# Cross attention on one core: the tail copy moved between exp and high part, and a third buffer for the low parts

## The reference

```python
q = (pre_q @ Wq + bq).reshape(b, ql, H, D_Q)
k = (pre_k @ Wk + bk).reshape(b, kl, H, D_Q)
v = (pre_k @ Wv + bv).reshape(b, kl, H, D_Q)
scores = jnp.einsum('bqhd,bkhd->bhqk', q, k) / jnp.sqrt(jnp.float32(D_Q))
attn = jax.nn.softmax(scores, axis=-1)
ctx = jnp.einsum('bhqk,bkhd->bqhd', attn, v).reshape(b, ql, H * D_Q)
out = ctx @ Wo + bo
x = pre_q + out
mu = jnp.mean(x, axis=-1, keepdims=True)
var = jnp.mean(jnp.square(x - mu), axis=-1, keepdims=True)
return (x - mu) * jax.lax.rsqrt(var + EPS) * gamma + beta
```

## Time and profile before

| | us |
|---|---|
| median of 3 runs (lowest, highest) | 908.91 (907.51, 912.77) |
| the profiled execution's own time | 911.81 |
| its span, first to last instruction | 909.9 |
| mean granted TensorE clock | 0.993 of full |
| TensorE matmuls busy | 882.5 |
| VectorE busy | 814.9 |
| ScalarE busy | 746.3 |
| GpSimd busy | 327.0 |

### The profile page before, as it was taken

How to read it: one execution, slowest core, us unless ns; L and a number is a source line. 1 busy time by engine, 2 the same in 40 slices (tenths; PEclk the granted TensorE clock), 3 DMA queues, 4 the chain that set the end, 5 groups by cost and what they waited for, 6 DMA issues and landing times.

```text
span 909.9 us, 25457 instructions
## 1 busy us (share of the span) xinstructions
PE 882.5 (97%) x10366; PEld 674.6 (74%) x10366; DVE 814.9 (90%) x1041; ACT 746.3 (82%) x1082; POOL 327.0 (36%) x385
## 2 busy tenths in 40 slices
PE   7799999999999999999999999999999999999996
PEld 6477777777777777777777777777777777777776
DVE  4799799999998999999899999989999899998983
ACT  3677868888888888888888888888888888888883
POOL 3032496434415234242514434143442435243011
PEclk9899999999999999999999999999999999999999
DMA  8598978999999999999999999999999999999995
GB/s 232 112 190 168 196 158 184 218 207 185 216 211 205 209 210 213 197 201 222 204 209 208 209 210 219 207 194 208 213 221 207 198 217 200 205 197 211 203 178 113
DMA packets 683065, 181.17 MB, mean 199 GB/s; under 512 B 654596, under 2 KB 682052, under 8 KB 682948
## 3 DMA queue, kind: packets, MB, share of 16 engines
q1 hardware_dynamic: 681332, 178.48, 103.7%
q10 hardware_dynamic: 1344, 0.53, 0.2%
q0 software_dynamic: 272, 0.53, 0.2%
HBM read 15.35 MB, written 0.82 MB: 18 GB/s over the span
## 4 chain that ended last, share of the span: by engine, by line
PE 34%; DVE 18%; ACT 15%; SPq 14%; DMA 11%; issue 8%; POOL 0%; POOLq 0%; ACTq 0%; DVEq 0%
PE ps L532 14%; PE ps L546 10%; DMA pt_lo<-p_lo 9%; DVE p_lo L767 8%; ACT p L861 6%; SPq L331 5%; DVE nmax L752 5%; PE ps L551 5%; ACT p_hi L869 5%; SPq L339 4%; PE ps L400 2%; ACT o_t L884 2%; DVE rsum L758 1%; SPq L323 1%; DMA pt_hi<-p_hi 1%
## 5 line engine op out<-in xcount | busy, mean ns | idle before, releaser
L869 ACT ACTIVATE p_hi<-p,rinv 128x1444 f16<-128x1444 f32 x200 | 299.8, 1499 | 89.3 <-DVE rinv L760 87.4
L767 DVE SCALAR_TENSOR_TENSOR p_lo<-p,rinv,p_hi 128x1444 f16<-128x1444 f32 x200 | 349.9, 1749 | 13.5 <-DMA pt_lo<-p_lo 10.7
L752 DVE TENSOR_REDUCE nmax<-ps 128x1 f32<-128x1446 f32 x200 | 329.8, 1649 | 8.7 <-PE ps L532 8.7
L861 ACT ACTIVATE p<-ps,nmax 128x1446 f32<-128x1446 f32 x200 | 291.7, 1459 | 26.3 <-DVE nmax L752 25.4
L546 PE MATMUL ps<-pt_hi,c_hi 128*128 128x128 f16 (+1 forms) x2288 | 268.7, 217 | 3.6 <-ACT o_t L884 3.1
L546 PE MATMUL ps<-pt_hi,c_lo 128*128 128x128 f16 (+1 forms) x2288 | 268.6, 217 | 0.0
L546 PEld LDWEIGHTS ps<-pt_hi,c_hi 128*128 128x128 f16 x2288 | 216.8, 98 | 34.4 <-ACT o_t L884 14.5
L546 PEld LDWEIGHTS ps<-pt_hi,c_lo 128*128 128x128 f16 x2288 | 217.0, 98 | 17.9 <-issue 0.2
L532 PE MATMUL ps<-ct_hi,g_hi 128*128 128x482 f16 (+3 forms) x624 | 157.1, 370 | 2.2 <-DMA ct_hi<-c_hi 2.2
L551 PE MATMUL ps<-pt_lo,c_hi 128*128 128x128 f16 (+1 forms) x2288 | 157.0, 217 | 0.0
L532 PE MATMUL ps<-ct_hi,g_lo 128*128 128x482 f16 (+3 forms) x624 | 156.8, 369 | 0.0
(11 more groups left out here) (109 smaller groups left out, 716.9 us busy)
## 6 DMA issues: line engine op xcount, KB each, us to landing
c_raw<-in_ctx_dram SPq DMA_DIRECT2D x32, 256.0 KB
pt_hi<-p_hi SPq DMA_TRANSPOSE x200, 3.5
pt_lo<-p_lo SPq DMA_TRANSPOSE x200, 3.8
c_raw<-in_ctx_dram SPq DMA_DIRECT2D x16, 192.0 KB
c_raw<-in_ctx_dram SPq DMA_DIRECT2D x48, 18.0 KB
out_dram<-late_sb SPq DMA_DIRECT2D x16, 50.0 KB
x_sb<-in_x_dram SPq DMA_DIRECT2D x1, 600.0 KB
o_t<-in_L_xattn_Wq_dram SPq DMA_DIRECT2D x2, 256.0 KB, 4.5
```

What stands on the lines that cost most here:

```text
L752: dve.tensor_reduce(nmax[:, n % RING:n % RING + 1], ps[:, bank:bank + 3, 0:KEYW], AX.XY, ALU.max, negate=True).then_inc(s_nm, 1)
L767: dve.scalar_tensor_tensor(out=p_lo[:, par, 0:KL], in0=p32[:, n % P32S, 0:KL], scalar=rinv[:, i:i + 1], in1=p_hi[:, par, 0:KL], op0=ALU.mu ...
L861: act.activation(p32[:, n % P32S, :].rearrange("p (k w) -> p k w", w=KEYW), ps[:, bank:bank + 3, 0:KEYW], ACT.Exp, bias=nmax[:, i:i + 1], ...
L869: act.activation(p_hi[:, par, 0:KL], p32[:, n % P32S, 0:KL], ACT.Copy, scale=rinv[:, i:i + 1]).then_inc(s_hi, 1)
```

## The change

Four things are changed.

1. p_lo has three buffers (LOS = 3) instead of two, with a semaphore each. The tail copy and the low part wait for the low transfer of tile n - 3.
2. ScalarE makes the tail copy of tile n - 1 between exponentials(n) and hi_part(n), instead of the tail copy of n behind hi_part(n).
3. In tiles 0 to 3 ScalarE empties its prologue banks ahead of exponentials(n), and VectorE its own behind row_max(n) and ahead of lo_part(n - 1), instead of at the end of the tile.
4. The bank J_X1 is emptied by VectorE instead of ScalarE.

```diff
--- before.py
+++ after.py
@@ -40,6 +40,7 @@
     SCOREW = 3 * KEYW
     LAG = 4
     PTS = 3
+    LOS = 3
     LOADS = 6
     TG = 4
     NT = KT // TG
@@ -93,6 +94,10 @@
     def halves(n):
         return 16 * (n // 2 + 1)
 
+    def turns(n):
+
+        return 16 * (n // LOS + 1)
+
     with ExitStack() as es:
         def sb(name, shape, dt=F32):
             return es.enter_context(nc.sbuf_tensor(name, shape, dt))
@@ -102,7 +107,7 @@
 
         sb("pad_to_256_bytes", [P, 32])
         p_hi = sb("p_hi", [P, 2, KT * P], F16)
-        p_lo = sb("p_lo", [P, 2, KT * P], F16)
+        p_lo = sb("p_lo", [P, LOS, KT * P], F16)
         pt_hi = sb("pt_hi", [P, PTS, KT - 1, P], F16)
         pt_lo = sb("pt_lo", [P, PTS, KT, P], F16)
         c_hi = sb("c_hi", [P, 2, KT, D], F16)
@@ -225,7 +230,7 @@
         s_pt = sem("p_hi_tail_ready")
         s_lo = sem("p_lo_ready")
         s_th = [sem(f"p_hi_transposed{i}") for i in range(2)]
-        s_tl = [sem(f"p_lo_transposed{i}") for i in range(2)]
+        s_tl = [sem(f"p_lo_transposed{i}") for i in range(LOS)]
         s_pv = sem("pv_ready")
         s_ot = sem("o_t_ready")
         s_fin = sem("output_projected")
@@ -245,7 +250,7 @@
         J_M0, J_M1, J_M2, J_M3, J_R = range(J_X3 + 1, J_X3 + 6)
         N_PRO = J_R + 1
         J_M = (J_M0, J_M1, J_M2, J_M3)
-        BY_SCALAR = [1, 3, J_A + 1, J_A + 2, J_A + 3, J_X, J_V0, J_X1, J_V1, J_M1, J_M3]
+        BY_SCALAR = [1, 3, J_A + 1, J_A + 2, J_A + 3, J_X, J_V0, J_V1, J_M1, J_M3]
         BY_VECTOR = [k for k in range(N_PRO) if k not in BY_SCALAR]
         ONCE = {0: (J_V0, J_X1), 1: (J_V1, J_X2), 2: (J_X3,),
                 8: (J_M0,), 9: (J_M1,), 10: (J_M2,), 12: (J_M3,), 17: (J_R,)}
@@ -336,7 +341,7 @@
                 sp.wait_ge(s_pt, n + 1)
                 if n >= PTS:
                     sp.wait_ge(s_pv, segments_before(n - PTS + 1))
-                sp.dma_start_transpose(pt_lo[:, n % PTS, :, :], p_lo[:, par, :]).then_inc(s_tl[par], 16)
+                sp.dma_start_transpose(pt_lo[:, n % PTS, :, :], p_lo[:, n % LOS, :]).then_inc(s_tl[n % LOS], 16)
 
             def store(b):
                 sp.wait_ge(s_y, b + 1)
@@ -545,7 +550,7 @@
                         for c in (c_hi, c_lo):
                             pe.matmul(out_t, c[:, b % 2, t, :], pt_hi[:, n % PTS, t, at:at + rows],
                                       start=(t == 0 and c is c_hi), stop=False)
-                    pe.wait_ge(s_tl[par], halves(n))
+                    pe.wait_ge(s_tl[n % LOS], turns(n))
                     for t in range(KT):
                         c = c_hi[:, b % 2, t, :] if t < KT - 1 else c_tail[:, b % 2, :]
                         mm = pe.matmul(out_t, c, pt_lo[:, n % PTS, t, at:at + rows], start=False, stop=(t == KT - 1))
@@ -762,9 +767,9 @@
             def lo_part(n):
                 par, i = n % 2, n % RING
                 dve.wait_ge(s_hi, n + 1)
-                if n > 1:
-                    dve.wait_ge(s_tl[par], halves(n - 2))
-                dve.scalar_tensor_tensor(out=p_lo[:, par, 0:KL], in0=p32[:, n % P32S, 0:KL], scalar=rinv[:, i:i + 1],
+                if n >= LOS:
+                    dve.wait_ge(s_tl[n % LOS], turns(n - LOS))
+                dve.scalar_tensor_tensor(out=p_lo[:, n % LOS, 0:KL], in0=p32[:, n % P32S, 0:KL], scalar=rinv[:, i:i + 1],
                                          in1=p_hi[:, par, 0:KL], op0=ALU.mult, op1=ALU.subtract).then_inc(s_lo, 1)
 
             def take_queries(b, g):
@@ -788,6 +793,10 @@
             for n in range(N + 1):
                 if n < N:
                     row_max(n)
+                if n < LAG:
+                    for k in ONCE.get(n, ()):
+                        if k in BY_VECTOR:
+                            empty(k)
                 if n >= 1:
                     lo_part(n - 1)
                 if n == N:
@@ -796,9 +805,10 @@
                 w, r = window(n)
                 if r == ROWS_AT and w > 0:
                     take_rows(w - 1)
-                for k in ONCE.get(n, ()):
-                    if k in BY_VECTOR:
-                        empty(k)
+                if n >= LAG:
+                    for k in ONCE.get(n, ()):
+                        if k in BY_VECTOR:
+                            empty(k)
                 if n < NT:
                     context_max(1, n)
                 elif n == FIRST_TOP:
@@ -870,10 +880,10 @@
 
             def hi_tail(n):
                 par, i = n % 2, n % RING
-                if n > 1:
-                    act.wait_ge(s_tl[par], halves(n - 2))
+                if n >= LOS:
+                    act.wait_ge(s_tl[n % LOS], turns(n - LOS))
                 tail = p32[:, n % P32S, (KT - 1) * P:KL].unsqueeze(1).to_broadcast([P, 2, KTAIL])
-                act.activation(p_lo[:, par, KL:KL + 2 * KTAIL].rearrange("p (i k) -> p i k", i=2), tail, ACT.Copy,
+                act.activation(p_lo[:, n % LOS, KL:KL + 2 * KTAIL].rearrange("p (i k) -> p i k", i=2), tail, ACT.Copy,
                                scale=rinv[:, i:i + 1]).then_inc(s_pt, 1)
 
             def take_result(n):
@@ -887,18 +897,24 @@
             for n in range(N + LAG):
                 if n >= LAG:
                     take_result(n - LAG)
+                else:
+                    for k in ONCE.get(n, ()):
+                        if k in BY_SCALAR:
+                            empty(k)
                 if n < N:
                     exponentials(n)
+                if 1 <= n <= N:
+                    hi_tail(n - 1)
                 if n >= N:
                     continue
                 hi_part(n)
-                hi_tail(n)
                 w, r = window(n)
                 if r in CHI_AT and w + 1 < B:
                     context_hi(w + 1, CHI_AT.index(r))
-                for k in ONCE.get(n, ()):
-                    if k in BY_SCALAR:
-                        empty(k)
+                if n >= LAG:
+                    for k in ONCE.get(n, ()):
+                        if k in BY_SCALAR:
+                            empty(k)
                 if A16_AT <= n < A16_AT + NG:
                     g = n - A16_AT
                     act.wait_ge(s_axs, 2)
```

## The result

| | before | after |
|---|---|---|
| median of the runs (lowest, highest; number) | 908.22 (907.25, 912.77; 6) | 903.32 (902.63, 904.62; 6) |
| the profiled execution's own time | 911.81 | 902.63 |
| its span | 909.9 | 900.7 |
| mean granted TensorE clock | 0.993 | 0.989 |

The ratio of the times is 0.9936, with an interval of 0.9911 to 0.9961: the kernel became 4.9 us faster, and 902.0 was 1.3 us too low.

What follows compares the result with a forecast made beforehand. TensorE was taken as full at 3.74 us a bare tile, so only its standing time could be won. 1.7 (start) + 0.25 (m_sb copy) + 5.2 (o_t waits), about 7.2 us, gave 904.6 profiled, median 902, range 897 to 907.5.

Steps and rivals of the forecast that it cites:

- the third buffer: p_lo: waiting for the transfer three tiles back removes 15.3 and 10.7 us of waits; TensorE gains 5.2 us.
- The signs named ahead as right: Stall near 30 us gone, tile 4 scores near 38.2, p_lo waits near zero, exp to exp 3.74, few o_t waits.
- Two signs named as wrong: High parts waiting for pt_hi transfers; SyncE waiting for the tail copy with the high transfer behind it.
- The start: Prologue: emptying banks early removes TensorE's stall at 30.05 and brings VectorE's chain forward; 1.7 us, between 0 and 3.2.
- The m_sb copy: The job at 75.71 waits 2.03 us for ScalarE's copy, which now stands ahead of the tail; 0.25 us won.
- J_X1 to VectorE for nothing: Prologue: one copy of some 0.5 us moves to VectorE while it waits for exp of tile 0; no cost.
- The waits for o_t: TensorE's 28 weight-load waits for late output copies fall to a few; 5.2 us won, between 3.1 and 7.6.
- the two readings of the 2.9 us over the median: Profiled run's excess: profiling cost, giving median 901.7, or more late transfers, giving 903 to 904; 902 taken.
- Rival 1: Near 130 us VectorE's low part takes the shared port before GpSimd's addition; 3.8 us won, 898; chance 0.12.
- Rival 2: ScalarE's wait moves to p_hi's two buffers; only 0.5 of the 5.2 us left, 906.5; chance 0.18.
- Rival 3: Late tail blocks SyncE's in-order issue, so high transfers go out later; 5 us slower, 914; chance 0.07.
- Rival 4: TensorE is not full and ScalarE's cycle sets every tile; 50 us won, 859; chance 0.01.

Runs made afterwards that it cites:

- e5: The changed kernel with two p_lo buffers instead of three: 902.58 us, ratio 0.9933 to the kernel before.
- e3: The kernel before with only the new order of the prologue banks (J_X1 by VectorE, banks emptied early): 906.72 us, ratio 0.9987.
- e7: The changed kernel with GpSimd's output bias addition in eight pieces spread over batches: 898.45 us, ratio 0.9886 to the kernel before.
- e2: The kernel before with only the tail copy moved between exp and high part, two p_lo buffers: 903.23 us, ratio 0.9957.
- e6: The changed kernel with the next batch's context maxima made in tiles 0 and 1 instead of 0 to 2: 900.80 us, ratio 0.9911 to before.
- e1: The kernel before with only the third p_lo buffer: 905.13 us, ratio 0.9980.
- e10: e8 with two p_lo buffers instead of three: 897.39 us, ratio 0.9878 to the kernel before.
- e4: The changed kernel with GpSimd's bias addition cut into eight in a row, row step waiting for its own piece: 900.42 us, ratio 0.9926 to before.
- e9: e8 with a third p_hi buffer: 896.06 us, ratio 0.9892 to the kernel before.
- e8: The changed kernel with both the early maxima of e6 and the spread pieces of e7: 897.96 us, ratio 0.9905 to the kernel before.

## Why the prediction was right or wrong

**The mechanism was right, but for the part given to the third buffer.** The signs named ahead as right are there, but for the scores of tile 4, which came sooner than 38.2: the stall near 30 us gone, exp to exp 3.74, no wait of ScalarE for p_lo, 3 o_t waits instead of 28, 0.18 us left of the 0.42 (about 0.1 was said), tile 11 no longer at 76.8. Two signs named as wrong are there too, high parts that wait for pt_hi's transfer and SyncE that waits for the tail copy, and both turned out to cost nothing (rivals 2 and 3 below). The sum of 7.2 stands against 9.2 in the profiled pair and 5.2 between the two second profiles (906.6 and 901.4).

**The start: right in size, unsure in cause.** 1.7 us were predicted at tile 10, with tile 4's scores near 38.2. Where the scores of tile 0 ran at half clock, as in the profile of before, that is what came: 38.31 for tile 4 and 67.99 for tile 10 in e5, 38.44 and 68.18 in e3, against 69.8 in the three profiles of the old order, 1.6 to 1.8 us. In other runs the low clock fell earlier, as these rows of before and of after show (window, its length, busy time of five engines, granted clock, DMA share, GB/s):

```profile
10.00:20.00 10.00, 7.32 (x70) 6.86 (x69) 7.84 (x17) 5.49 (x12) 4.78 (x8) 1.00 1.03 256
20.00:24.00 4.00, 3.50 (x10) 1.50 (x11) 0.00 (x0) 0.45 (x1) 3.33 (x5) 0.59 0.32 73
```

```profile
10.00:20.00 10.00, 9.35 (x61) 8.68 (x61) 6.50 (x15) 4.95 (x10) 4.70 (x7) 0.66 1.02 254
20.00:24.00 4.00, 3.29 (x21) 2.08 (x22) 1.76 (x3) 1.24 (x3) 3.45 (x6) 1.00 0.36 72
```

Then tile 4 is reached at 36.98, 1.3 us sooner than in e5, but tile 10 at 67.89, about as in e5. Most of the lead goes in one wait of VectorE, in tile 5:

```profile
43.33 0.37 ACT L894 ACTIVATE o_t<-ps,unscale 128x128 f32<-128x128 f32 x1 [1.94 <-PE ps L556]
...
45.18 0.15 DVE L763 TENSOR_SCALAR rsum<-psums 128x1 f32<-128x1 f32 x1 [0.99 <-ACT p L871]
```

Behind the stall of 4.11 us the scores of tile 4 and part of the product behind them run at half clock. ScalarE waits 1.94 us for that product, its exp of tile 5 is late, and VectorE, which sets the pace here, stands 0.99 us for it. The second profile of the changed kernel has 1.17 us and e7 1.24; without this wait tiles 4 to 10 take 29.9 us in all three. In e5 the half clock ends sooner (its third group of tile 4 takes 0.78 us again) and VectorE has no such wait.

And e2, with the old order at the start but this better clock, has tile 10 at 67.83 too. No profile shows the old order at the better clock without the moved tail, so there the start order's share can't be told from the clock's. The clock is not the change's: the changed kernel and e5, alike up to a buffer, have it on different sides. Compared at the same clock, e5 and before are 2.2 us apart at tile 11 (74.61 and 76.79), where 1.95 were predicted.

**The m_sb copy: under-sized.** 0.25 us was said; tile 10 to 11 is 0.25 shorter in e2, which has only the moved tail, 0.21 in e3, which has only the start, 0.41 in e5 with both, and 0.6 in the changed kernel.

**J_X1 to VectorE for nothing: right only through another stall.** TensorE now stands 0.96 us for VectorE's xT copy at 29.11, a wait that I had not in the sum. It costs nothing, because the long stall before tile 4 follows and ends when VectorE has the maxima. That stall is the step that I left alone ("TensorE's stall before tile 4 stays"): it stayed, it grew to 4.11, and e6 shows that it was worth more than the whole start edit, 2.2 us in the median and 2.5 at tile 11, for maxima that stand a tile earlier. The half clock behind it was not foreseen either; it costs nothing up to tile 10 where it is short (4 to 10 takes 29.68 in e5 and 29.79 in before), and 1.0 to 1.2 us where it lasts through tile 4's scores, as told above.

**The waits for o_t: the mis-sized term, and the wrong name.** The 5.2 was worked out from one profile (and is called the middle of 3.1 and 7.6, which is 5.35). Against it the stretch from 25 to 199 gained 6.5 in the first pair of profiles and 2.4 in the second. How many transfers are late differs from run to run in the kernel before (28 and 20 waits), and the profile I had was one with many. Of the two readings of the 2.9 us over the median I took the one that profiling costs it; the second profile of before says the other, and the sentence "the new one would stay near 903 to 904" is what happened. The second pair (from two chips), whose 5.2 is nearest to the median's 4.9, has 2.5 up to tile 11, 2.4 from 25 on, and 0.3 at the end.

And the credit went to the third buffer. e1 and e2 each remove these waits, or nearly all, alone, e5 loses nothing without the buffer, e10 neither. The copy now starts 5.18 us behind its own tile's exp (3.74, and 251.25 less 249.81) instead of 3.38 (253.82 less 250.44), so the transfer that it waits for has had 1.8 us more. With the tail moved, the buffer only takes VectorE's waits away, 18.8 us (e5), which lie in its slack.

**Rival 1 (the lock order) happened and won nothing.** VectorE was first, as that case needs, and the low part took 1.71 us. The 3.8 us did not come, since a dependence on data lay under the lock: the row step needs what the addition makes. I had read "<-DVE late_sb" as the low part's queue alone. e4 and e7 then won that stall by taking the dependence away, e7 4.6 us by the median, 4.2 of them from tile 22 to 25. In e4 a third of it (2.8 won instead of 4.2) was lost again while VectorE waited beside GpSimd's pieces. The Trainium skill ("SBUF — State Buffer", SBUF: two separate sides) has the one who comes first keep the port for its whole instruction. The trace of before agrees for a single instruction, and e4 shows 4.47 us against a row of eight that start 0.69 us apart. By a lock that changes hands between two instructions the low part would have come in after the piece under way at 134.32, which ends at 134.65, and ended by about 136.4, an estimate from these rows; it ended at 138.79.

**Rival 2 (the wait moves to p_hi)**: the waits did move, 1.9 to 15.4 us, and cost nothing, as e9 shows. **Rival 3**: SyncE did wait for the late tail:

```profile
SPq L343 <- ACT p_lo L886: 33.4, 51, 4.2
```

33.4 us in 51 waits, and that costs TensorE nothing either: 25 tiles take 105.87. **Rival 4** is out: the cycle of ScalarE shrank and the bare tile stayed at 3.74.

Open stay why the low clock falls at tile 0, at 10 to 20 us, before that (e8), or at 74 to 84 us, and so how much of the 1.9 us between the medians of e1 and e2 is the edit: their profiles differ by 3.6 us, 3.3 of it in two stretches that had lower clock in e1 (0 to 4 by 1.62, 11 to 22 by 1.65), 0.26 at tile 10 and 0.25 at the end.

The best versions are e7, e8, e9 and e10, at 0.988 to 0.9905 of the kernel before, where the changed kernel has 0.9928 to 0.9936: 2 to 5 us less. Their ratios do not set these four apart. Of the three with both later edits, e10 needs the fewest buffers.

## What to carry to other kernels

A wait of an engine that feeds the bound one costs only where that engine falls behind by more than its slack; 18.8 us of VectorE's waits for p_lo and 15.5 us of ScalarE's for p_hi were worth nothing here, while ScalarE's 11.7 to 15.3 us of waits for p_lo, on its longer cycle, cost 3 to 6.5 us (tiles 25 to 199 of the two profiles of before against e1). Before adding a buffer, see whether the instruction that waits can stand later in its engine's list: here that did the same. Take two profiles of the kernel before and compare them stretch by stretch between the same instructions, and when a lock's order is to change, first look whether the one who waits also needs the other's result.

## What the runs showed of the hardware

- Eight GpSimd additions in a row (5.51 us) kept a VectorE instruction with two SBUF inputs from its work as one long one does: 4.47 us for 1.71 (e4). With the first piece alone at that place the low part takes 1.71 us again (e7). It is so the other way round too: a GpSimd copy beside a low part took 1.70 us, and 0.29 without one, as the rows at 127.38 (after) and 129.63 (before) show.
- The low clock of the prologue falls in different places in kernels whose prologues are alike: 0.66 granted from 10 to 20 us in after, 0.57 from 20 to 24 us in e5, which differs by one buffer. In e8 the column of the granted clock shows 1.00 from 10 to 20 us, while the matmuls take twice their time (3.57 us for 1.95). There the lengths of the matmuls tell the clock, and the column does not.
- Idle time of 4.1 us ahead of tile 4 was followed by scores at half clock (after, e3, e5), idle time of 2.9 us there was not in before and e2. But in e1 the same 2.9 us was: the second of tile 4's three groups takes 1.38 us, where the first takes 0.79. Idle time of 3.1 to 3.3 us ahead of tile 2 was followed by half clock (e2, before). So the length of the idle time alone does not tell it.
